# A routed feed-forward layer around attention: first layer's tiles grouped by batch, two batches' attention set between its last tiles

## The chip, the cores and the metric

One core of a Trainium2 chip. The metric is the time of one execution on the device in microseconds, median over several runs. Its engines are TensorE (PE in the profile, with its weight loads as PEld), VectorE (DVE), ScalarE (ACT), GpSimd (POOL) and the queue of SyncE (SP), which only issues transfers here.

## The reference

The input x is 4 batches of 256 tokens with 512 features, float32. Three steps are added to x in turn:

```python
x = x + 0.5 * ffn(layernorm(x), W_gate, b_gate, W_e, b_e)
x = x + attn(layernorm(x), Wqkv, bqkv, Wo, bo)
x = x + 0.5 * ffn(layernorm(x), W_gate, b_gate, W_e, b_e)

def ffn(x, W_gate, b_gate, W_e, b_e):        # 8 experts, 512 -> 512
    logits = x @ W_gate + b_gate
    _, top_idx = jax.lax.top_k(logits, 2)    # two experts for a token, equal weight
    y_all = relu(einsum('bsd,edh->bseh', x, W_e) + b_e)
    return take_along_axis(y_all, top_idx[..., None], axis=2).mean(axis=2)

def attn(x, Wqkv, bqkv, Wo, bo):             # one head of 128, within a batch
    q, k, v = split(x @ Wqkv + bqkv)
    return softmax(q @ k.T / sqrt(128)) @ v @ Wo + bo
```

Both feed-forward layers have the same weights. A token's attention needs the first layer's result for every token of its own batch, and for no other batch.

## The kernel before

The 1024 tokens are 8 row tiles of 128 (two for a batch); x stays in SBUF. Three phases follow one another.

**First layer.** For each batch, x is normalised, transposed, multiplied by the gate's weights (`gate`), and the two best experts of each token are found (`choose`). The 2048 pairs of token and expert are ranked within their expert by matmuls with a triangle of ones (`count`, `split_rank`). `tile_starts`, `slots` and `in_tiles` then put the pairs of one expert into tiles of 128 rows, expert after expert, over all batches together; `row_hots` and the matmuls of `token_list` turn this round into a list of tokens for each of NS = 23 tiles (16 would hold the pairs, 7 more allow for the partly filled last tile of each expert). `tokens` writes the list, and only then can the first gather start. `tile_experts` writes each tile's expert.

Each of the 23 tiles of `experts` is: a gather of 128 normalised rows from DRAM by POOL (`gather`), four transposes on PE, a split into a high and a low part (ACT's `hi_rows`, DVE's `lo_rows`), 12 matmuls of 128x512 (high by high, high by low, low by high), the bias on DVE (`bias`), ReLU on ACT (`relu`), and a scatter of the rows to `z_dram` (`scatter`). The expert weights (8 MB) stream in meanwhile; the last six half-loads wait until the first two gathers have landed (L401 to L404), and ACT and DVE split them in two parts (`split_hi`, `split_lo`). PE, ACT and DVE run tiles 8 to 19 in a loop.

**Attention.** All scatters of the first layer come first, since an expert's tiles hold tokens of all batches. Then DVE adds the two halves of z to x (`add_z`), takes the moments (`moments`), POOL raises the variance to the power -1/2 (`deviations`), DVE normalises, and PE, ACT and DVE pass through the four batches: transposes, `project_qk`, `project_v`, `scores`, maximum and exponential (`score_max`, `softmax`), `transpose_prob`, `mix_v`, `project_out`, `add_attention`. Every engine's order is written out by hand. Batch b's routing for the second layer (kind `g1`) stands between the steps of batches b+1 and b+2. The attention of one batch on PE is independent work for the waits of another. At the end of the phase an early list (`slots_early`, NA = 5 tiles filled from batches 0 to 2 alone) lets the second layer start before batch 3 is routed.

**Second layer.** As the first; batch 3's rows are transposed inside tile 0, gated after it, and its pairs listed by tile 3. Tiles from 5 on use the second list. At the end z is read back, added and stored.

PSUM has eight banks and all are used. `warm_up` issues matmuls whose results nobody reads. `WARM = [16, 10, 0]` stands behind the lists, `WARM_ATT = 14` ahead of the attention.

## Time and profile before

| | |
|---|---|
| time, median of 3 runs | 286.95 us (286.3 to 287.64) |
| time of the profiled execution | 283.61 us |
| its span, first to last instruction | 281.7 us |
| mean granted TensorE clock | 0.967 |
| PE busy | 240.1 us (85%) |
| DVE busy | 171.0 us (61%) |
| POOL busy | 120.4 us (43%) |
| ACT busy | 103.3 us (37%) |

The profiled execution took 1.9 us more than its span, which lie ahead of the first and behind the last instruction. All times below are microseconds from the start of the span. A busy PE here includes the unread matmuls of `warm_up`, so its share is not useful work alone; which engine sets the pace has to be read stage by stage.

### The profile page before, as it was taken

What the parts mean: (1) busy time and instruction counts of PE and PEld (TensorE: products, weight loads), DVE (VectorE), ACT (ScalarE), POOL (GpSimd) and SP (SyncE); (2) the same over time, 40 slices, a digit from 0 to 9 for tenths busy, and PEclk for the clock granted to TensorE, in tenths of its full rate; (3) what the DMA queues carried; (4) which work ended last, traced back from release to release, by engine and by line L of the source; (5) the groups of instructions that cost most, each with busy time, mean ns of one, the idle gap of its engine ahead of it and who ended that gap; (6) DMA issues with size and microseconds to landing.
All of it is one profiled execution on the core that took longest, in us unless ns stands there. A gap on an engine that the chain in (4) does not pass through costs nothing.

```text
span 281.7 us, 4837 instructions
## 1 busy us (share of the span) xinstructions
PE 240.1 (85%) x1302; PEld 178.2 (63%) x1303; DVE 171.0 (61%) x428; ACT 103.3 (37%) x184; POOL 120.4 (43%) x136
## 2 busy tenths in 40 slices
PE   6576788979999999989999968478969999999920
PEld 2342356758888888658786845246848888888710
DVE  3679947987344344775698785935843344443574
ACT  1888414554333333214244433013332433334200
POOL 4200373764656663324414400152076566664340
PEclk9999999999999999999999988689999999999995
DMA  7999249994444346353401011063056444454598
GB/s 241 387 391 411 79 131 353 416 381 129 147 151 137 132 150 198 108 154 100 149 3 74 20 58 74 1 176 124 0 168 203 134 134 147 152 147 152 213 370 315
DMA packets 22790, 49.38 MB, mean 175 GB/s; under 512 B 4333, under 2 KB 4973, under 8 KB 22513
## 3 DMA queue, kind: packets, MB, share of 16 engines
q1 hardware_dynamic: 13712, 26.55, 25.9%
q0 software_dynamic: 7360, 20.46, 22.8%
q10 hardware_dynamic: 1696, 2.11, 2.1%
q8 instruction: 11, 0.18, 0.3%
q14 instruction: 11, 0.08, 0.1%
HBM read 34.42 MB, written 18.35 MB: 187 GB/s over the span
## 4 chain that ended last, share of the span: by engine, by line
PE 58%; DMA 14%; DVE 12%; issue 5%; ACT 4%; SPq 2%; POOL 1%; DVEq 1%; POOLq 0%; ACTq 0%
PE qk_ps L845 17%; PE y_ps L845 17%; PE tp_ps L821 5%; PE qk_ps L916 5%; DMA xg<-xn_dram,tok 4%; DMA xg_late<-xn_dram,tok 4%; PE tp_ps L758 3%; DMA whi<-z_dram 3%; PE v_ps L925 3%; DMA raw<-in_L_ffn_W_e_dram 2%; DMA x<-in_L_attn_x_dram 2%; DVE row_hot L1144 2%; PE sp_ps L950 1%; DVE stats L1048 1%; PE rk_ps L745 1%
## 5 line engine op out<-in xcount | busy, mean ns | idle before, releaser
L514 POOL DMA_INDIRECT z_dram<-yrow,place x23 | 26.4, 1149 | 29.3 <-ACT yrow L637 26.7
L506 POOL DMA_INDIRECT xg<-xn_dram,tok x23 | 24.8, 1080 | 28.0 <-DVE tok L1193 20.8
L506 POOL DMA_INDIRECT xg_late<-xn_dram,tok x23 | 22.6, 981 | 33.0 <-DVE tok L1193 22.9
L1269 DVE TENSOR_TENSOR xt_lo_late<-tp_ps,xt_hi_late 128x512 fp32r<-128x512 f32 x23 | 15.9, 691 | 26.9 <-ACT xt_hi_late L627 26.9
L1269 DVE TENSOR_TENSOR xt_lo<-tp_ps,xt_hi 128x512 fp32r<-128x512 f32 x23 | 15.9, 691 | 24.2 <-ACT xt_hi L627 24.2
L637 ACT ACTIVATE yrow<-ypre 128x512 f32<-128x512 f32 x22 | 13.9, 632 | 43.4 <-DVE ypre L1277 43.4
L514 POOL DMA_INDIRECT z_dram<-xn,place x16 | 17.9, 1116 | 17.9 <-ACT xn L637 17.0
L499 POOL TENSOR_TENSOR rstd<-var_eps,neg_half 128x2 f32<-128x2 f32 x12 | 8.8, 737 | 32.4 <-DVE var_eps L1055 32.4
L358 DVE TENSOR_TENSOR wlo<-raw,whi 128x1024 fp32r<-128x1024 f32 x16 | 19.0, 1216 | 0.5 <-ACT whi L572 0.5
L637 ACT ACTIVATE xn<-ypre_late 128x512 f32<-128x512 f32 x14 | 8.8, 632 | 27.6 <-DVE ypre_late L1277 27.6
L1048 DVE BATCH_NORM_STATS2 stats<-x 128x6 f32<-128x512 f32 x24 | 15.7, 684 | 4.4 <-DMA x<-in_L_attn_x_dram 4.2
L627 ACT ACTIVATE xt_hi_late<-tp_ps 128x512 fp32r<-128x512 f32 x23 | 13.4, 583 | 11.3 <-PE tp_ps L821 11.3
L572 ACT ACTIVATE whi<-raw 128x1024 fp32r<-128x1024 f32 x16 | 16.3, 1048 | 1.6 <-DMA raw<-in_L_ffn_W_e_dram 1.6
L821 PE MATMUL tp_ps<-ident,xg_late 128*128 128x128 f32 x92 | 13.8, 274 | 3.2 <-DMA xg_late<-xn_dram,tok 3.2
L845 PE MATMUL y_ps<-whi,xt_hi 128*128 x48 | 14.5, 423 | 2.0 <-ACT xt_hi L627 1.1
L821 PE MATMUL tp_ps<-ident,xg 128*128 128x128 f32 x92 | 14.0, 275 | 2.1 <-DMA xg<-xn_dram,tok 2.1
L821 PEld LDWEIGHTS tp_ps<-ident,xg_late 128*128 128x128 f32 x92 | 11.0, 140 | 7.3 <-DMA xg_late<-xn_dram,tok 3.6
L627 ACT ACTIVATE xt_hi<-tp_ps 128x512 fp32r<-128x512 f32 x23 | 13.4, 581 | 6.2 <-PE tp_ps L821 6.2
L845 PE MATMUL y_ps<-whi,xt_hi_late 128*128 x48 | 14.4, 421 | 1.2 <-ACT xt_hi_late L627 1.2
L916 PE MATMUL qk_ps<-xt_att,wqkv 128*128 128x256 f32 x64 | 14.9, 386 | 0.4 <-ACT xt_att L611 0.4
L821 PEld LDWEIGHTS tp_ps<-ident,xg 128*128 128x128 f32 x92 | 11.0, 140 | 6.6 <-DMA xg<-xn_dram,tok 4.4
L745 PE MATMUL sp_ps<-ones 128*128 128x512 bf16 x50 | 14.2, 430 | 0.0
(177 smaller groups left out, 537.8 us busy)
## 6 DMA issues: line engine op xcount, KB each, us to landing
raw<-in_L_ffn_W_e_dram SPq DMA_DIRECT2D x16, 512.0 KB, 9.1
z_rows<-z_dram SPq DMA_DIRECT2D x6, 512.0 KB, 3.7
x<-in_L_attn_x_dram SPq DMA_DIRECT2D x8, 256.0 KB, 4.7
be_bc<-in_L_ffn_b_e_dram SPq DMA_DIRECT2D x2, 1024.0 KB, 12.0
xn_dram<-xn ACTq DMA_DIRECT2D x8, 256.0 KB, 2.1
whi<-z_dram SPq DMA_DIRECT2D x4, 512.0 KB, 5.4
wlo<-z_dram SPq DMA_DIRECT2D x4, 512.0 KB, 7.8
out_dram<-x SPq DMA_DIRECT2D x8, 256.0 KB, 3.3
```

Of the source, the lines that this page charges most:

```text
L358: eng.tensor_tensor(half(wlo, n), half(raw, n), half(whi, n).bitcast(F32), ALU.subtract).then_inc(done, 1)
L506: pool.indirect_dma_start(out=xg_at(f, t % XG), out_offset=None, in_=xn_dram[f][0:T - S if f and t < NA else T, :], in_offset=bass.Indirec ...
L514: pool.indirect_dma_start(out=z_dram[f][:, :], out_offset=bass.IndirectOffsetOnAxis(ap=place[:, t:t + 1], axis=0), in_=yrow_at(f, t % YB), ...
L572: act.activation(half(whi, n), half(raw, n), ACT.Copy).then_inc(hi_made, 1)
L627: act.activation(xt_hi_at(f, t % 2), tp_ps[(n0 + t) % 2][:], ACT.Copy).then_inc(tp_copied, 1)
L637: act.activation(yrow_at(f, t % YB), ypre_at(f, t % 2) if t < NY[f] else y_ps[t % 2][:], ACT.Relu, scale=HALF_MEAN).then_inc(yrow_made, 1)
L745: pe.matmul(bank[:], ones[:], ones[:].unsqueeze(1).broadcast_to([P, 4, P]), start=True, stop=True)
L821: last = pe.transpose(tp_ps[(n0 + t) % 2][:, c * P:(c + 1) * P], xg_at(f, t % XG)[:, c * P:(c + 1) * P], ident[:])
L845: last = pe.matmul(y_ps[t % 2][:], rows[:, c * P:(c + 1) * P], w[:, bass.ds(e * WE + c * H, H)], start=(n == 0), stop=(rows is lo and c == ...
L916: last = pe.matmul(qk_ps[:, j * S:(j + 1) * S], wqkv[:, c, j * D:(j + 1) * D], xt_att[:, c, :], start=(c == 0), stop=(c == NC - 1))
L1048: read.append(step(dve.bn_stats(stats[:, s + i, :], x[:, TB * b + i, :])))
L1269: dve.tensor_tensor(xt_lo_at(f, t % 2), tp_ps[(n0 + t) % 2][:], xt_hi_at(f, t % 2).bitcast(F32), ALU.subtract).then_inc(xt_made, 1)
```

## The change

- The first layer's pairs go into tiles by groups: first the tiles that batch 0 opens, expert after expert, then those that batch 1 opens beyond them (a pair fills up the expert's open tile first), then batch 2, then batch 3. `group_slots(0, 3)` computes this for three batches ahead of the last batch's `choose`, and `group_slots(3, 4)` for the last behind it. They replace `tile_starts(0)` and `slots(0)`. `tile_experts(0)` compares with the ends of 32 groups instead of 8.
- The rows of z for a batch are read as soon as the scatters of its groups have landed; SP waits on counts in `sent_rows`. They are read by 256 KB into two row slots of `xn`, one after the other.
- The attention of batch 0 starts in tile 16 of the first layer and that of batch 1 in tile 20, in pieces on PE, ACT and DVE inside and behind tiles. Its buffers lie in `xt_gate` and in the last batch's part of x, which SP loads again from the input afterwards.
- The first layer is written out in full on PE, ACT and DVE, with no loop.
- After the first layer come batch 2's attention, the second layer's routing of batches 0, 1 and 2, and batch 3's projections; the early list stands ahead of batch 3's softmax, so its gathers go out beside the rest of batch 3's attention. `project_out(3)` is then the last step before the second layer's first tile.
- The unread matmuls go: 14 + 2 ahead of the attention, 10 behind the early list.

The core of the diff:

```diff
+    EARLY = 2
+    START = (16, 20)
...
-        WARM = [16, 10, 0]
-        WARM_ATT = 14
+        WARM = [16, 0, 0]
...
-        HEADS, STEP = (E, NA), 6
+        HEADS, STEP = (NS, NA), 6
...
+                def attention_inside(t):
+                    for b in range(EARLY):
+                        if t == START[b]:
+                            transpose_xn("att", b)
+                        if t == START[b] + 1:
+                            project_v(b)
+                            scores(b)
+                        if t == START[b] + 2:
+                            transpose_prob(b)
+                        if t == START[b] + 3:
+                            project_out(b)
+
+                def attention_behind(t):
+                    for b in range(EARLY):
+                        if t == START[b]:
+                            project_qk(b)
+                        if t == START[b] + 2:
+                            mix_v(b)
...
             experts(0)
+            transpose_xn("att", 2)
+            project_out(1)
+            project_qk(2)
+            project_v(2)
+            scores(2)
+            transpose_xn("g1", 0)
+            transpose_prob(2)
+            mix_v(2)
+            project_out(2)
+            gate(1, 0)
+            transpose_xn("g1", 1)
+            transpose_logits(1, 0)
+            gate(1, 1)
+            count(1, 0)
+            transpose_logits(1, 1)
+            transpose_xn("g1", 2)
+            transpose_xn("att", 3)
+            count(1, 1)
+            gate(1, 2)
+            project_qk(3, 0, 1)
+            transpose_logits(1, 2)
+            project_qk(3, 1, 2)
+            project_v(3)
+            count(1, 2)
+            scores(3)
             token_list(1)
+            transpose_prob(3)
+            mix_v(3)
+            project_out(3)
             experts(1)
...
+            def group_slots(first, end):
+
+
+                n = end - first
+                cols = slice(JB * first, JB * end)
+                pairs = JB * n
+                counts = group_at[:, first + 1:end + 1, 1, :]
+                dve.tensor_tensor(above[:, 0:n], upto[:, first:end, :].unsqueeze(3).broadcast_to([P, n, E, NT]),
+                                  thresh[:].unsqueeze(1).broadcast_to([P, n, E, NT]), ALU.is_gt
+                                  ).then_inc(rank_read, n)
+                dve.wait_ge(rank_read, B + end if end == B else B - 1 + n)
+                link(dve.tensor_reduce(counts, above[:, 0:n], AX_X, ALU.add))
+                link(dve.tensor_tensor(group_new[:, first:end, :], counts, group_at[:, first:end, 1, :], ALU.subtract))
+                link(dve.tensor_tensor_scan(ends[:, 0:end, :].rearrange("p b e -> p (b e)"),
+                                            group_new[:, 0:end, :].rearrange("p b e -> p (b e)"),
+                                            zeros(end * E), 0.0, ALU.add, ALU.add))
...
+                link(dve.tensor_tensor(
+                    hot, onehot[:, TB * first:TB * end].rearrange("p t k e -> p (t k) e").unsqueeze(2)
+                    .broadcast_to([P, pairs, 2 * end, E]),
+                    group_at[:, 1:end + 1].rearrange("p b c e -> p (b c) e").unsqueeze(1)
+                    .broadcast_to([P, pairs, 2 * end, E]), ALU.mult))
+                link(dve.tensor_reduce(of_pair, hot, AX_X, ALU.add))
...
+            split_rank(0, 2)
+            group_slots(0, B - 1)
             choose(0, 3)
-            split_rank(0, 2)
             row_hots(0, 2)
-            tile_starts(0)
-            slots(0)
+            split_rank(0, 3)
+            group_slots(B - 1, B)
+            in_tiles(0, slot_t[:])
+            row_hots(0, 3)
             tokens(0)
             tile_experts(0)
...
             experts(0)
+            normalise("att", 2)
+            dve.wait_ge(x_att, TB)
+            moments("g1", 0)
+            add_attention(1)
+            normalise("g1", 0)
+            dve.wait_ge(x_att, TB * 2)
+            moments("g1", 1)
+            add_bv(2)
+            normalise("g1", 1)
+            score_max(2)
+            add_z(6)
+            add_z(7)
+            moments("att", 3)
+            invert_sums(2)
+            add_attention(2)
+            dve.wait_ge(x_att, TB * 3)
+            moments("g1", 2)
+            normalise("att", 3)
+            choose(1, 0)
+            normalise("g1", 2)
+            split_rank(1, 0)
+            row_hots(1, 0)
+            choose(1, 1)
+            split_rank(1, 1)
+            row_hots(1, 1)
+            choose(1, 2)
+            add_bv(3)
             slots_early()
+            row_hots(1, 2)
+            score_max(3)
             tokens(1)
+            tile_experts(1)
+            invert_sums(3)
+            add_attention(3)
             dve.wait_ge(x_att, TB * B)
+            moments("g1", 3)
+            normalise("g1", 3)
             leave_early()
             experts(1)
```

## Rows read from the trace of the kernel before

**Rows 1.** The page, granted clock in 40 slices of the span.

```profile
PEclk9999999999999999999999988689999999999995
```

**Rows 2.** Windows: length, busy of each engine, granted clock, DMA share, GB/s.

```profile
118.14:129.40 11.26, 10.00 (x59) 7.23 (x57) 7.85 (x19) 2.52 (x5) 3.06 (x5) 1.00 0.60 188
129.40:162.60 33.20, 32.73 (x194) 26.34 (x193) 25.53 (x65) 14.10 (x35) 12.80 (x12) 1.00 0.16 58
162.60:190.79 28.19, 19.45 (x118) 11.97 (x117) 18.69 (x77) 6.17 (x14) 5.48 (x6) 0.82 0.25 77
190.79:210.70 19.91, 16.38 (x106) 11.91 (x104) 13.30 (x48) 7.03 (x13) 7.41 (x8) 1.00 0.28 89
```

**Rows 3.** Windows around the clock's fall (columns as in rows 2).

```profile
165.10:167.83 2.73, 0.28 (x4) 0.04 (x2) 2.55 (x9) 1.02 (x4) 0.70 (x1) 0.96 0.00 0
167.83:171.10 3.27, 3.27 (x14) 3.18 (x15) 1.29 (x13) 1.55 (x3) 0.00 (x0) 0.51 0.32 122
```

**Rows 4.** Timeline of DVE and POOL, first list: start, length, instruction, idle before.

```profile
22.30 0.22 DVE L1082 TENSOR_REDUCE logit<-g_ps 128x16 f32<-128x64 f32 x1
...
23.61 0.18 DVE L1111 TENSOR_TENSOR picked<-onehot,rk_ps 128x32 f32<-128x32 bf16 x1
...
25.07 0.22 DVE L1082 TENSOR_REDUCE logit<-g_ps 128x16 f32<-128x64 f32 x1
...
32.40 0.33 DVE L1152 TENSOR_TENSOR passed<-iota_t,incl 1x184 f32<-1x184 f32 x1
...
32.79 1.18 POOL L506 DMA_INDIRECT xg<-xn_dram,tok  x1 [20.78 <-DVE tok L1193]
...
33.22 3.47 DVE L358 TENSOR_TENSOR wlo<-raw,whi 128x1024 fp32r<-128x1024 f32 x3
...
34.27 3.25 POOL L506 DMA_INDIRECT xg<-xn_dram,tok  x1 [0.31 <-issue]
```

**Rows 5.** Timeline of DVE and ACT: operations by size, and the steps of a softmax.

```profile
142.16 0.69 DVE L1384 TENSOR_REDUCE smax<-sp_ps 128x2 f32<-128x512 f32 x1 [0.53 <-PE sp_ps L934]
...
143.09 0.47 ACT L685 ACTIVATE prob<-sp_ps,nmax 128x256 f32<-128x256 f32 x1 [1.09 <-DVE nmax L1385]
...
146.54 0.60 ACT L727 ACTIVATE pt<-sp_ps 128x512 f32<-128x512 f32 x1
...
177.44 0.36 DVE L1218 TENSOR_TENSOR picked_a<-onehot,bounds 128x192 f32<-128x192 bf16 x1
```

**Rows 6.** The chain that ended last: start, length, engine and line.

```profile
39.95 5.31 DMA raw<-in_L_ffn_W_e_dram
...
111.75 2.78 PE qk_ps L845 x12
...
140.38 0.87 PE tp_ps L758 x8
...
142.12 3.65 PE qk_ps L916 x16
145.78 0.44 PE sp_ps L942 x4
146.21 1.79 PE v_ps L925 x16
...
149.74 0.86 PE y_ps L962 x2
```

**Rows 7.** Timeline of DVE and POOL ahead of the second layer.

```profile
176.28 0.18 DVE L1111 TENSOR_TENSOR picked<-onehot,rk_ps 128x32 f32<-128x32 bf16 x1
...
179.22 0.68 DVE L1144 TENSOR_TENSOR row_hot<-iota_r,slot_r 128x512 bf16<-128x512 bf16 x1
...
180.95 1.28 DVE L1048 BATCH_NORM_STATS2 stats<-x 128x6 f32<-128x512 f32 x2
...
184.17 0.74 POOL L499 TENSOR_TENSOR rstd<-var_eps,neg_half 128x2 f32<-128x2 f32 x1
...
185.04 1.00 DVE L1075 TENSOR_SCALAR xn<-x,mv,rstd 128x512 f32<-128x512 f32 x2 [1.77 <-POOL rstd L499]
```

More of the change, by code:

```diff
@@ L315, in xn_slot @@
         def xn_slot(n):
-            return n if n < NT else n % XN
+            if n < NT:
+                return n
+            return n % TB if n < NT + EARLY * TB else (n + TB) % XN
         def xn_at(n):
@@ L1150, in tile_experts @@
                 first, tiles, _, _ = LISTS[n]
-                ends = bounds[0:1, 1, :] if n == 1 else incl[0:1, :]
-                link(dve.tensor_tensor(passed[:, 0:tiles], iota_t[0:1, 0:tiles].unsqueeze(2).broadcast_to([1, tiles, E]),
-                                       ends.unsqueeze(1).broadcast_to([1, tiles, E]), ALU.is_ge))
-                link(dve.tensor_reduce(eid_f[:, first:first + tiles], passed[:, 0:tiles], AX_X, ALU.add))
-                dve.tensor_scalar(eid[:, first:first + tiles], eid_f[:, first:first + tiles], float(E - 1), None,
-                                  ALU.min).then_inc(eid_made, 1)
+                part = slice(first, first + tiles)
@@ new lines, in tile_experts @@
+                if n == 0:
+                    hot = row_hot[0:1].rearrange("p j r -> p (j r)").bitcast(F32)[:, 0:NS * B * E].rearrange(
+                        "p (t e) -> p t e", t=NS)
+                    passing = ends[0:1].rearrange("p b e -> p (b e)")
+                else:
+                    hot = passed[:, 0:tiles]
+                    passing = bounds[0:1, 1, :] if n == 1 else incl[0:1, :]
+                of_all = hot.shape[2]
+                link(dve.tensor_tensor(hot, iota_t[0:1, 0:tiles].unsqueeze(2).broadcast_to([1, tiles, of_all]),
+                                       passing.unsqueeze(1).broadcast_to([1, tiles, of_all]), ALU.is_ge))
@@ L1274, in bias, with attention @@
                     dve.wait_ge(exp_done, done)
-                    if used is not None:
+                    if f == 0:
+                        if t >= YB:
+                            dve.wait_ge(scattered[t % YB], 16 * (t // YB))
+                    else:
                         dve.wait_ge(yrow_made, used)
-                    dve.tensor_tensor(ypre_at(f, t % 2), y_ps[t % 2][:],
+                    dve.tensor_tensor(ypre_at(f, t), y_ps[t % 2][:],
                                       be_bc[:, bass.ds(e * H, H)], ALU.add).then_inc(ypre_made, 1)
                 halves = list(range(LO_AHEAD, 2 * E)) if f == 0 else []
+                def attention(t):
+                    if t == START[0] - 4:
+                        add_z(0)
+                    if t == START[0] - 3:
+                        add_z(1)
+                    if t == START[0] - 2:
+                        moments("att", 0)
+                    if t == START[0] - 1:
+                        normalise("att", 0)
+                        add_bo(0)
+                    if t == START[0]:
+                        add_z(2)
+                        score_max(0)
+                    if t == START[0] + 1:
+                        add_bv(0)
+                        add_z(3)
+                    if t == START[0] + 2:
+                        invert_sums(0)
+                        moments("att", 1)
+                    if t == START[1] - 1:
+                        normalise("att", 1)
+                        add_attention(0)
+                    if t == START[1]:
+                        add_z(4)
+                        score_max(1)
+                    if t == START[1] + 1:
+                        add_bv(1)
+                        add_bo(1)
+                        add_z(5)
+                    if t == START[1] + 2:
+                        moments("att", 2)
+                        invert_sums(1)
                 def tile(t):
@@ new lines, in add_z @@
+                for m in range(TOP_K * i, TOP_K * (i + 1)):
+                    last = m - TOP_K * (NT - TB)
+                    if last < 0:
+                        dve.wait_ge(z_in[m % 2], 16 * (m // 2 + 1))
+                    else:
+                        dve.wait_ge(z_last[last], 16)
+                    if m % TOP_K:
+                        dve.wait_ge(z_added, m)
+                    dve.tensor_tensor(x[:, i, :], x[:, i, :], z_row(m), ALU.add).then_inc(z_added, 1)
+            bo_steps = {}
@@ new lines, in invert_sums, with add_attention @@
+            def invert_sums(b):
+                dve.wait_ge(prob_made, TB * (b + 1))
+                link(dve.reciprocal(pinv[:], psumrow[:]))
+            def add_attention(b, first=0, end=TB):
+                for q in range(first, end):
+                    i = TB * b + q
+                    if b < EARLY:
+                        dve.wait_ge(dve_step, bo_steps[i])
+                    else:
+                        dve.wait_ge(bo_added, i - TB * EARLY + 1)
+                    dve.wait_ge(wo_done, i + 1)
+                    dve.scalar_tensor_tensor(out=x[:, i, :], in0=wo_bank(b, q)[:], scalar=pinv[:, q:q + 1],
+                                             in1=x[:, i, :], op0=ALU.mult, op1=ALU.add).then_inc(x_att, 1)
```

612 lines of the change are left out of this document (312 added, 300 removed).

## The prediction

> **What bounds the kernel now.** I read the page's clock row first, then a table of windows, the chain that ended last, and the timelines of the stretches that the change touches. In the clock row [rows 1] the reader is to see one valley in the middle of the span. The windows [rows 2] place it. From 129.40 to 162.60 PE is busy 32.73 of 33.20 us: three batches' attention, each filling the other's waits, at full clock. Ahead of it, from 118.14 (the first layer's last matmul) to 129.40, its 10.00 busy us contain 16 unread warm-up matmuls. Behind it, from 162.60 to 190.79 (the end of the second layer's tile 0), PE is busy 19.45 of 28.19 us at a mean clock of 0.82, ten warm-ups included; the work there is half of one batch's attention, the early list and one tile. So some 20 us of the 72.65 us from 118.14 to 190.79 are latency. The first layer's later tiles are bound by PE: 2.78 us for 12 matmuls [rows 6], with 0.44 us of transposes between, and nothing else on the chain. The first list is bound by DVE: until 32.79, when the first gather goes out, one DVE operation follows the other [rows 4].
>
> **The sum's base** is the profiled execution, 283.61 us. The median of the runs is 286.95, 3.3 us above it; the difference found below is added to the median. A difference of 0.5% is 1.4 us, about what a measurement can tell here.
>
> **The first list grows.** All of it stands on DVE's chain to the first gather. An operation on 192 elements takes 0.36 us, one on 512 takes 0.69 [rows 5]; on that line 576 elements cost 0.76, 256 cost 0.43, 64 cost 0.23, and the smallest ones 0.18 [rows 4]. Each has some 0.03 us to the next.
> - `group_slots(0, 3)`: 192 elements compared and summed (2 x 0.39), a product of 12 pairs by 6 groups by 8 experts = 576 elements and its sum (2 x 0.79), seven small ones with a scan (7 x 0.20): 3.8 us.
> - `group_slots(3, 4)`: 64 elements twice (0.5), 256 elements twice (0.9), seven small ones (1.4): 2.8 us.
> - Out go `tile_starts(0)` and `slots(0)`, whose own part is 1.1 us (an estimate: two operations on 128 elements and four small ones).
>
> Net 5.5 us. `choose` (22.30 to 23.61, 1.3 us) and rank with row marks (23.61 to 25.07, 1.5 us) [rows 4] change places and keep their costs. `tile_experts(0)` also grows, from 184 to 736 elements, twice, about 1.4 us, but behind the gather's issue. Is the delay hidden later? The last six half-loads of weights wait for the first two gathers, and the chain has one of them at 39.95 for 5.31 us [rows 6]; they move with the list. So the whole first layer moves: +5.5. Bounds: +3.5 if the second gather slips ahead of DVE's weight splits and the loads go out earlier; +6.8 if the splits' own delay of 1.4 is added.
>
> The second of these bounds is visible in one pair of rows: the gather issued at 34.27 took 3.25 us, the one before it 1.18, and DVE split weights for 3.47 us from 33.22 [rows 4]. The Trainium skill, page "SBUF — State Buffer", the section "SBUF: two separate sides", has GpSimd write its descriptors through a port pair that VectorE holds for a whole instruction in its fast modes; that agrees with the 3.25 us. By that rule the second gather ends only with the later splits, and the sum would be 1.4 us higher; by the row alone it may pass as the first one did.
>
> **Attention between the tiles.** One batch on PE is, by the chain [rows 6]: transposes 0.87, query and key 3.65, value 1.79, scores 0.87, probabilities transposed 0.44, mix 0.87, projection 2 x 0.86: 10.2 us. Batch 0 brings all, batch 1 all but the mix and projection (2.6) by the end of tile 22: 17.8 us. Following DVE's order through tiles 15 to 20 I find two stalls. In tile 16 the second transpose waits for `lo_rows(17)`, which stands behind `bias(15)`, `normalise` (1.00, [rows 7]) and `add_bo` (two of 0.65): 1.1 us. In tile 20 it waits likewise behind `normalise` and `add_attention`: 1.2 us. Everything else is covered: maximum 0.69 and two exponentials of 0.47 [rows 5] lie beside 3.2 us of matmuls. Are z's rows there? I counted the reference's routing on its inputs: the tiles opened end at 8, 12, 16 and 19, so batch 2 is complete with tile 15 and its rows are first added in tile 20. Tile 22 ends 20.2 us later than without the pieces (17.8 + 2.3, and 0.1 of small waits).
>
> **From tile 22 to the second layer's tile 0.** PE's work there, piece by piece in the order of the diff with the prices above (gates 0.57 and lists 0.6 as estimates): 33.6 us. I followed the five engines' orders step by step; PE waits
> - 2.7 ahead of batch 2's transposes: `moments` (1.28 and some small ones) starts on DVE only after `add_bv`, `add_bo` and `add_z(5)` of tile 21, then POOL's 0.74 and the normalisation follow [rows 7];
> - 1.9 for batch 2's probabilities, since `score_max(2)` stands behind `add_bv(2)` and `normalise("g1", 1)`; 1.2 in its two copies by ACT (0.60 and about 0.4, [rows 5]);
> - 2.9 for `choose(1, 0)` and `choose(1, 1)`, behind four `add_z`, two `moments`, and `add_attention`;
> - 3.1 for the early list: `slots_early` takes 2.94 (176.28 to 179.22, [rows 7]) and starts only when batch 3's value is projected and `add_bv(3)` done;
> - 1.6 and 1.2 for batch 3's probabilities and copies, with the softmax now behind the list;
> - 1.9 around tile 0, where batch 3's moments and normalisation, begun after `project_out(3)`, are no longer early.
>
> These make 16.5, and 1.2 us of small waits: 51.3 us where before 72.65 passed. DVE is busy 39 of the 51: it is the engine that sets this stage. The first gather of the second layer is covered, as meant. Saved: 21.3.
>
> **Clock.** Before, PE was nearly idle for 2.73 us (165.10 to 167.83), and the next 3.27 us of work ran at 0.51 of full clock [rows 3], half of them lost: 1.6 us. The new order has two such gaps, 2.7 and 3.1 us, and no unread matmuls to bridge them, each followed by work on the path: 2 x 1.6 = +3.3 (bounds: 0, and 7 if the clock stays down through the sparse part).
>
> **Sum:** +5.5 + 20.2 - 21.3 + 3.3 = +7.6 us. The second layer's tiles 1 to 4 keep their chain of waits, 16.38 busy of 19.91 us [rows 2]. 283.61 becomes 291.2, and the median 286.95 becomes 294.5. Own range of this case: 289 to 300.
>
> **Rivals.**
> - *The new order hides its own waits.* For it: the dense stretch, where hand-ordered pieces left 0.5 us idle in 33.2 [rows 2]. Against it: DVE had 7.7 us to spare there, and here has 39 busy us in 51. If half of the 20 us (16.5 waits and 3.3 clock) goes, the time is 284.5; if all, 275. It decides, as faster than before by 1.4, once 9 of these 20 are gone.
> - *The clock holds* across both gaps: 291.2.
> - *The clock stays down* from the gate of batch 0 to `project_out(3)`: some 15 us of PE work, spread over 25, at half clock; half of the extra 15 falls into waits, so +7 instead of +3.3 and the later tiles start cold: 300 to 302. For it: one gap was enough before. Against it: work came back to 1.00 after each. The Trainium skill, "TensorE: Matmul & The Clock Gate", Part 1, says that the gate follows how busy the engine was lately; the fall after 2.73 idle us agrees, and it would make a stage as sparse as this the wrong place to drop warm-ups.
> - *The growth of the list is swallowed*, because the weights set the pace of tiles 2 to 6: 289. Against it: their loads are released by the gathers.
> - *The interleaving does not work*: rows of z land late, each `add_z` stalls DVE and then PE. With two row slots and a read back issued only after the addition before last, four late reads of 3 us make 305. The counts speak against it.
>
> **Chances.** Forecast 0.45, order hides its waits 0.20, clock holds 0.13, clock stays down 0.10, growth swallowed 0.08, interleaving fails 0.04. Faster: the second case and an edge of the mild ones, 0.22. Within 0.5%: 0.08. Slower: 0.70. The range takes half of the faster case and the cold one: 282 to 302.
>
> **What would show it.** The first gather at 38.2 and not 32.8; tile 22 ending near 144; pieces of attention inside tiles 16 to 22 with PE busy over 95%; gaps of 2 to 3 us ahead of batch 2's transposes and of the early list's matmuls, with granted clock 0.5 behind them; tile 0 of the second layer ending near 198. I am wrong if the gather leaves before 36, or if DVE idles long after tile 22 while PE is dense, or if tile 0 ends before 190.

## The result, and the profile after

The changed kernel takes 304.18 us (median of 4 runs, 303.28 to 306.0), the kernel before 286.72 us beside it. The ratio is 1.070, with a 95% interval of 1.063 to 1.077; the two medians alone give 1.061, the two profiled executions 1.070. Which of the two is nearer isn't settled, but both are far beyond the spread of the runs. Below, ratios leave out executions in a slower state that any kernel here sometimes falls into, while medians are of all runs. The prediction had 294.5 us and a range up to 302: the direction is right, the size is not. The profiled execution took 303.42 us; its span of 301.3 us is 19.6 longer than before, where the forecast had 7.6.

The page's clock row of the changed kernel, in the place of [rows 1]:

```profile
PEclk9998699999999979999979686959999999999995
```

One valley became many: the first list (slices 4 and 5), tile 16 (slice 15), and four stretches after tile 22 (slices 21, 23, 24 with 25, and 27). The windows, in the place of [rows 2]: first tile 12's first matmul to the end of tile 22, then to the end of the second layer's tile 0, then its next tiles.

```profile
89.21:147.74 58.53, 55.25 (x278) 44.94 (x277) 32.55 (x60) 19.40 (x40) 21.66 (x21) 0.97 0.35 109
147.74:210.96 63.22, 45.56 (x236) 31.59 (x236) 39.29 (x135) 15.98 (x35) 14.56 (x15) 0.81 0.21 68
210.96:230.30 19.34, 15.76 (x103) 11.59 (x102) 13.30 (x48) 6.43 (x12) 6.91 (x7) 1.00 0.33 107
```

In the middle row PE is busy for 45.56 of 63.22 us at a clock of 0.81; DVE's 39.29 us are what the prediction had (39). The cold stretches by themselves, each with the granted clock in the third column from the right:

```profile
106.60:110.00 3.40, 2.98 (x9) 2.56 (x10) 0.32 (x2) 0.60 (x1) 1.55 (x2) 0.53 0.44 149
151.10:154.30 3.20, 3.18 (x10) 2.40 (x11) 2.00 (x6) 1.19 (x2) 1.26 (x2) 0.52 0.20 53
164.90:171.30 6.40, 5.24 (x11) 2.91 (x12) 3.20 (x9) 2.07 (x4) 0.70 (x1) 0.50 0.22 82
178.80:185.00 6.20, 5.67 (x33) 4.22 (x34) 4.81 (x25) 2.78 (x5) 0.00 (x0) 0.50 0.23 87
195.80:202.20 6.40, 4.50 (x10) 2.69 (x11) 0.69 (x5) 1.67 (x6) 2.00 (x2) 0.50 0.29 82
```

That is 25.6 us at the lower of the clock's two levels, with 21.6 us of PE work in them, where before one such stretch held 3.27 us of work [rows 3], and one more the ten unread matmuls behind the early list. What PE waited for from tile 22 to tile 0 (total, times, longest):

```profile
PE tp_ps L841 <- DVE xn L1193: 4.5, 3, 2.5
PE sp_ps L1060 <- ACT prob L769: 3.9, 2, 2.3
PE v_ps L895 <- ACT mark_a L683: 2.4, 1, 2.4
PE g_ps L856 <- DVE logit L1200: 2.0, 1, 2.0
PE sp_ps L1068 <- ACT pt L777: 1.4, 2, 0.7
```

These are the waits of the forecast, in its places: ahead of batch 2's transposes (2.5, forecast 2.7), for the probabilities of batches 2 and 3 (2.3 and 1.6; forecast 1.9 and 1.6), for the early list (2.4; forecast 3.1), for `choose` (2.0 and 0.5 us; forecast 2.9 together). In all PE is idle for 17.7 us of this stretch, in sum the forecast's 17.7; what the forecast lacked is mostly the speed of the work between the waits.

Where the 19.6 us of the span are, by the same landmarks in both traces:

| | before | after | difference | forecast |
|---|---|---|---|---|
| start to tile 12's first matmul | 82.6 | 89.2 | +6.6 | +5.5 |
| tile 12 to the end of tile 22 | 35.6 | 58.5 | +23.0 | +20.2 |
| end of tile 22 to the end of tile 0, second layer | 72.65 | 63.22 | -9.4 | -18.0 (-21.3 + 3.3) |
| the rest | 90.9 | 90.3 | -0.6 | 0 |

The stretch behind tile 0 is the same work in all variants of the changed kernel, and its length lay between 90.3 and 92.5 us in their traces. Differences of a microsecond or two between single traces are therefore not read where nothing was changed.

The second row's surplus begins in tile 16. DVE's timeline of the changed kernel there, then PE's:

```profile
98.01 1.49 DVE L1539 TENSOR_TENSOR x<-x,xn 128x512 f32<-128x512 f32 x2 [1.73 <-DMA xn<-z_dram]
...
104.07 1.00 DVE L1193 TENSOR_SCALAR xn<-x,mv,rstd 128x512 f32<-128x512 f32 x2 [0.41 <-POOL rstd L564]
104.99 1.29 DVE L1545 TENSOR_TENSOR x<-x,bo_bc 128x512 f32<-128x512 f32 x2
106.19 0.68 DVE L1437 TENSOR_TENSOR xt_lo<-tp_ps,xt_hi 128x512 fp32r<-128x512 f32 x1
```

```profile
104.67 0.66 PE L841 MATMUL tp_ps<-ident,xn 128*128 128x128 f32 x4 [0.50 <-DVE xn L1193]
107.02 1.08 PE L841 MATMUL tp_ps<-ident,xn 128*128 128x128 f32 x4 [1.69 <-DVE xt_lo L1437]
107.76 2.05 PE L933 MATMUL y_ps<-whi,xt_lo 128*128 x4
```

The chain is read backwards: four matmuls took 2.05 us and not some 1.1 because the clock had fallen; the transposes ahead of them waited 1.69 us for `lo_rows(17)`; that stood behind the normalisation and `add_bo`, as forecast, but all of it was late, since DVE had waited 1.73 us for rows of z. Their read went out at 93.69, only when the addition before had freed the one buffer it needs.

### The profile page after: what moved, and what is told of

It reads as the page before. It is cut to its first block, busy times and chain, and to the rows that moved or that the text cites. A ratio compares the mean times of both kernels' runs of the same rounds, so it can differ in the third digit from the quotient of the medians.

```text
span 301.3 us, 4702 instructions
## 1 busy us (share of the span) xinstructions
PE 245.4 (81%) x1276; PEld 181.1 (60%) x1277; DVE 180.0 (60%) x454; ACT 104.1 (35%) x184; POOL 116.1 (39%) x133
## 4 chain that ended last, share of the span: by engine, by line
PE 48%; DVE 19%; DMA 15%; issue 6%; ACT 5%; POOL 2%; SPq 2%; DVEq 1%; POOLq 0%; ACTq 0%
PE qk_ps L933 14%; PE y_ps L933 12%; DMA be_bc<-in_L_ffn_b_e_dram 5%; PE tp_ps L907 4%; PE tp_ps L841 3%; DMA wlo<-z_dram 3%; PE qk_ps L1031 2%; PE g_ps L1031 2%; PE v_ps L1043 2%; DMA xg<-xn_dram,tok 2%; DVE xn L1193 2%; PE sp_ps L1068 2%; DVE stats L1166 1%; DMA xn<-z_dram 1%; DMA x<-in_L_attn_x_dram 1%
## 5 line engine op out<-in xcount | busy, mean ns | idle before, releaser
L571 POOL DMA_INDIRECT xg<-xn_dram,tok x23 | 26.8, 1166 | 34.2 <-DVE tok L1328 26.3
L703 ACT ACTIVATE yrow<-yrow 128x512 f32<-128x512 f32 x22 | 13.9, 632 | 41.6 <-DVE yrow L1448 41.6
L579 POOL DMA_INDIRECT z_dram<-xn,place x16 | 16.5, 1030 | 18.2 <-ACT xn L703 17.2
L841 PE MATMUL tp_ps<-ident,xn 128*128 128x128 f32 x80 | 14.6, 330 | 9.8 <-DVE xn L1193 5.0
L564 POOL TENSOR_TENSOR rstd<-var_eps,neg_half 128x2 f32<-128x2 f32 x12 | 8.8, 735 | 33.6 <-DVE var_eps L1173 33.6
L841 PEld LDWEIGHTS tp_ps<-ident,xn 128*128 128x128 f32 x80 | 11.0, 168 | 14.4 <-DVE xn L1193 6.5
L907 PE MATMUL tp_ps<-ident,xg_late 128*128 128x128 f32 x92 | 13.7, 273 | 2.8 <-DMA xg_late<-xn_dram,tok 2.8
```

What stands on the lines that cost most here:

```text
L571: pool.indirect_dma_start(out=xg_at(f, t % XG), out_offset=None, in_=xn_dram[f][0:T - S if f and t < NA else T, :], in_offset=bass.Indirec ...
L579: pool.indirect_dma_start(out=z_dram[f][:, :], out_offset=bass.IndirectOffsetOnAxis(ap=place[:, t:t + 1], axis=0), in_=yrow_at(f, t % YB), ...
L703: act.activation(yrow_at(f, t % YB), ypre_at(f, t) if t < NY[f] else y_ps[t % 2][:], ACT.Relu, scale=HALF_MEAN).then_inc(yrow_made, 1)
L841: last = pe.transpose(tp_ps[n % 2][:, c * P:(c + 1) * P], xn_at(m)[:, c * P:(c + 1) * P], ident[:])
L907: last = pe.transpose(tp_ps[use_no[(f"exp{f}", t)] % 2][:, c * P:(c + 1) * P], xg_at(f, t % XG)[:, c * P:(c + 1) * P], ident[:])
```

## The experiments

The kernel before was run beside each group of four; its runs there lie between 281.69 and 288.19 us, so times of different groups are compared through their ratio to it. Unless a sentence below says so, nothing of the computation is left out.

**1. The kernel before with a longer first list.** Operations of the sizes of `group_slots` are added to DVE's chain (192, 192, 576, 576 elements and small ones ahead of `choose(0, 3)`, 256, 256 and small ones behind it), results unread.

```diff
+            pad([192, 192, 8, 24, 8, 576, 576, 24, 24, 12, 12])
             choose(0, 3)
...
+            pad([32, 8, 256, 256, 12, 12])
             slots(0)
             tokens(0)
```

> The kernel before with 17 unused VectorE operations of the sizes of the groups' arithmetic set ahead of the first list (11 before the last batch's choice, 6 ahead of the slots), about 5.5 us of VectorE. If the first layer moves with its list, +5.5 us (291.3 to 292.5). If the weight loads set the pace of the first tiles and swallow the delay, under +2 us.

The first gather moved by 4.96 us (32.79 to 37.75), the end of tile 22 by 4.9 (118.14 to 123.04), the span from 281.7 to 286.7. Time 290.9 us, ratio 1.019 (1.008 to 1.030). In this trace every microsecond ahead of the first gather is one in the end: nothing swallows it. Its clock row dips to 7 in slice 5, where the row of before has 9, so the changed kernel's dip in the first list comes with the longer list.

**2. The same, with `tile_experts` longer by two operations of 552 elements.**

```diff
+            for n in (552, 552):
+                link(dve.tensor_tensor(scratch[:, 0:n], ...))
             tile_experts(0)
```

> As the run with the longer list, and two operations of 552 elements on one partition, 1.4 us, between the list and the tiles' experts. If the weight splits behind them hold up the second gather, and with it the last weight loads, this adds another 1.0 to 1.4 us (+6.6 in all, what the first layer of the changed kernel shows). If what stands behind the first gather's issue is covered, it adds under 0.3 us.

Tile 22 ended at 124.96, 6.8 us later than before and 1.9 later than in experiment 1; the ratio, 1.016 (1.006 to 1.026), doesn't separate the two. The way was not the expected one. POOL's gathers in this kernel:

```profile
38.20 1.37 POOL L506 DMA_INDIRECT xg<-xn_dram,tok  x1 [26.38 <-DVE tok L1193]
39.88 0.95 POOL L506 DMA_INDIRECT xg<-xn_dram,tok  x1 [0.31 <-issue]
41.13 3.31 POOL L506 DMA_INDIRECT xg<-xn_dram,tok  x1 [0.30 <-issue]
```

DVE's three splits ran from 40.14 to 43.6, so the second gather passed in 0.95 us and the third took 3.31. In the changed kernel the splits began at 39.82 and the second gather, at 39.91, took the blow:

```profile
39.91 4.22 POOL L571 DMA_INDIRECT xg<-xn_dram,tok  x1 [0.31 <-issue]
```

A gather that is issued beside the splits is held over all three of them: in both kernels, and in the kernel before (34.27, 3.25 us), it ends 0.8 us behind the last split. The Trainium skill, "SBUF — State Buffer", section "SBUF: two separate sides", has a VectorE operation with two inputs in SBUF hold a shared port pair for the whole instruction against a GpSimd operation that reads SBUF. These splits have two such inputs, and the traces agree, with 3.31 and 4.22 us beside 0.95, if a gather counts as such an operation; that no run here separates.

The layer was late by about as much in both kernels, but not for the same reason. In the changed kernel tile 1's transposes waited 0.97 us for the second gather's rows. Here the second gather passed and released the last weight loads at 43.46, ahead of the third gather, and tile 2's transposes waited for that one:

```profile
49.22 0.66 PE L821 MATMUL tp_ps<-ident,xg 128*128 128x128 f32 x4 [2.27 <-DMA xg<-xn_dram,tok]
```

(Experiment 7 shows this second way again.) So experiment 2 doesn't reproduce the changed kernel's delay. It does show that the prediction's lower bound of +3.5, where the second gather slips ahead of the splits and the loads go out earlier, isn't a gain. The changed kernel's own delay behind the first gather is read by comparing traces: from its first gather to tile 12's first matmul it takes 51.2 us, and 50.6 to 52.5 in experiments 4 to 6 and 9 to 11, against 49.3 to 49.8 in the kernel before and experiments 1, 3 and 12.

**3. The kernel before without its unread matmuls** between the layers: the 14 + 2 ahead of the attention and the 10 behind the early list, the same that the change drops.

```diff
-        WARM = [16, 10, 0]
+        WARM = [16, 0, 0]
...
-            warm_up(WARM_ATT)
...
-            warm_up(2)
```

> The kernel before without the 16 unread matmuls ahead of its attention and the 10 behind the early list. If the clock was a part of the price of the change, +2 to +5 us, with stretches at half clock behind 122 and 185. If the engine's waits alone set the pace there, within 1 us.

Time 289.71 us beside 287.07, ratio 1.015 (1.004 to 1.026); the span grew from 281.7 to 285.6. In the clock row the stretch of the first list is untouched and two places are new or deeper, at the start of the attention and ahead of the second layer:

```profile
PEclk9999999999999999959999998659999999999995
```

Without any of the rest of the change, this one edit costs 2.6 us by the medians and 3.9 by the spans. From the end of tile 22 to the end of tile 0 it is 78.2 us and not 72.65; the first layer and the rest came out 1.6 us shorter with nothing changed in them.

**4. The changed kernel with unread matmuls in every gap in which the clock fell.** 7 in tile 16 and as many in tile 20, 10 ahead of batch 2's transposes, 13 around its probabilities, 13 around `gate(1, 1)`, 20 from the early list to the mix of batch 3.

```diff
             experts(0)
+            pe.wait_ge(x_att, TB)
+            warm_up(10, rk_ps)
             transpose_xn("att", 2)
...
+            warm_up(9, rk_ps)
             transpose_prob(2)
+            warm_up(2, rk_ps)
             mix_v(2)
...
+            warm_up(8, qk_ps)
             gate(1, 1)
...
             scores(3)
+            warm_up(10, qk_ps)
             token_list(1)
+            warm_up(6, qk_ps)
             transpose_prob(3)
```

> The changed kernel with 5 to 10 unread matmuls in each of the gaps that its trace shows ahead of a fall of the clock (in tiles 16 and 20, ahead of batch 2's transposes, of its probabilities, of the second gate, of the third transposes, of the early list and of batch 3's probabilities). Theory of the clock: five cold stretches cost 10 us between them, and 6 to 10 us come back (294 to 298). Rival: VectorE's chain sets the pace and the half clock lies beside it; under 3 us come back (over 301).

Time 296.41 us, ratio 1.037 (1.025 to 1.049): 7.8 of the 17.5 us came back, or 3.3 of the 7.0 per cent, though the order of the real work is the same on every engine. The stage between the layers, as the middle row of the windows above:

```profile
147.36:202.38 55.02, 48.82 (x293) 31.22 (x292) 39.31 (x135) 15.64 (x35) 14.53 (x15) 1.00 0.25 78
```

55.0 us instead of 63.2, DVE's busy time unchanged, the clock at 1.00. The cost of the clock in this stage is therefore 8.2 us; the forecast had 3.3.

**5. Rows of z a tile sooner.**

```diff
-                    if t == START[0] - 4:
+                    if t == START[0] - 5:
                         add_z(0)
```

> The changed kernel with batch 0's rows of z added one tile sooner (in tile 11 and not in tile 12), so that their row slot is free and the next read goes out some 2.8 us earlier; all else as in the changed kernel, nothing left out. Theory: in tile 16 PE waited 1.7 us more than I had worked out and then ran 3.4 us at half clock because DVE had waited 1.73 us for the second pair of z rows. Then add_z(1) waits for nothing, the transposes of batch 0 wait about 1 us in tile 16, the clock keeps 1.0 there, tile 22 ends at 144.5 to 146 and not 147.7, and the time is 1.5 to 3 us under the changed kernel's: 301 to 302.7. Rival: the wait of tile 16 comes from lo_rows(17) standing behind the normalisation and add_bo, whenever the rows land: then tile 22 still ends at 147 or later, and the time falls by less than 1 us. Second rival: batch 0's own rows are not there a tile sooner, and the stall only moves: no gain or a loss up to 1 us.

301.39 us, ratio 1.056 (1.049 to 1.063). This interval only touches that of the changed kernel, and by the medians alone (301.39 over 284.7, 1.059 beside 1.061) next to nothing was gained, so the traces have to tell. From tile 12 to the end of tile 22 it is 55.8 us and not 58.5; in tile 16 PE waited once, for 1.22 us (forecast 1.1), and the clock stayed up:

```profile
104.08 0.60 PE L841 MATMUL tp_ps<-ident,xn 128*128 128x128 f32 x4
105.89 0.63 PE L841 MATMUL tp_ps<-ident,xn 128*128 128x128 f32 x4 [1.22 <-DVE xt_lo L1437]
106.28 1.17 PE L933 MATMUL y_ps<-whi,xt_lo 128*128 x4
```

So the late rows were the cause of the surplus of tile 16, and the rival falls. What is left, 20.3 us over before, is the forecast's 20.2, and in its parts: PE is busy 18.0 us longer than before (forecast 17.8) and waits 2.3 us in two places (forecast 2.3).

**6. Batch 3's softmax ahead of the early list**, on DVE, ACT and PE (ACT's line isn't shown).

```diff
             add_bv(3)
+            score_max(3)
             slots_early()
             row_hots(1, 2)
-            score_max(3)
...
             scores(3)
+            transpose_prob(3)
             token_list(1)
-            transpose_prob(3)
             mix_v(3)
```

> The changed kernel with batch 3's maximum and exponentials ahead of the early list on DVE and ACT, and its transposed probabilities ahead of token_list on PE; nothing left out. It undoes the order that lets the first gather of the second layer go out beside the rest of the attention. Theory: the list alone is 3 us of DVE work and PE has nothing meanwhile, so whichever goes first, the other waits; the two cold stretches behind 178.8 and 195.8 come from these two gaps. With the softmax first, PE has the mix and projection while DVE makes the list, one of the gaps closes, and tile 0's first product starts 1 to 3 us earlier unless its gather, which goes out later by about 1.2 us, sets its start: the time is 301 to 304 (0 to 3 us less). Rival: the early gather is what matters, its landing sets the start of tile 0; then the time rises by 1 to 3 us, to 305 to 307.

301.93 us, ratio 1.062 (1.053 to 1.071), against 1.070 (1.063 to 1.077): an overlap, so the times alone leave it open. In the trace tile 0 of the second layer starts its last product 59.7 us after the end of tile 22, and 62.0 us in the changed kernel (that product then ran at half clock here, so the ends are only 61.7 and 63.2). PE waited there for the list for 1.05 us and not 2.44. The gather that the change lets go early is not what tile 0 waits for here:

```profile
200.20 0.60 PE L907 MATMUL tp_ps<-ident,xg_late 128*128 128x128 f32 x4
201.63 1.19 PE L933 MATMUL y_ps<-whi,xt_hi_late 128*128 x4 [0.83 <-ACT xt_hi_late L693]
```

The transposes of its rows follow `project_out(3)` with no wait, as in the changed kernel. The order that the change chose for the list buys nothing and costs 1.5 to 2.3 us in this trace, with the clock as low as it is here; experiment 10 tries it with the clock held.

**7. The last six loads released by the first gather.**

```diff
-            for s in range(2):
-                sp.wait_ge(gathered[s], 16)
+            sp.wait_ge(gathered[0], 16)
```

> The changed kernel, but the last six half-loads of expert weights wait for the first gather alone and not for the first two; nothing left out. Theory: the first layer's delay is 6.6 us and not 5.5 because the second gather, blocked for 4.2 us while DVE splits weights, releases those loads at 46.55 and not at 45.5; released by the first gather they go out near 40 to 41, tile 4 to 6 are no longer late, and tile 12's first product starts 2 to 4 us earlier (85 to 87 and not 89.2), the time 2 to 4 us less. Rival: what holds tiles 2 to 6 is their gathers behind the splits and the broadcast of the tiles' experts and biases, not the loads; then tile 12 starts within 1 us of 89.2 and the time stays within 1 us; the gathers beside the loads may even take longer, with a loss up to 2 us.

305.48 us, ratio 1.072 (1.064 to 1.080). The loads went out at 42.85 instead of 46.55, and tile 16's first transposes came at 107.89 instead of 104.67 (0.9 of it because this run's first gather was at 38.96). The theory falls. The rival's last clause had the cause, that the gathers take longer beside the loads, though not its size:

```profile
45.33 1.07 PE L932 MATMUL y_ps<-wlo,xt_hi 128*128 x4
50.83 1.12 PE L906 MATMUL tp_ps<-ident,xg 128*128 128x128 f32 x4 [4.43 <-DMA xg<-xn_dram,tok]
51.60 2.06 PE L932 MATMUL y_ps<-whi,xt_lo 128*128 x4
```

The loads went out ahead of the second gather's rows; PE waited 4.43 us for these, and then ran at half clock. That gather left POOL at 45.06 and could be used at 50.8; in the changed kernel it left at 44.13 and was there at 46.5. With 3 MB of weights sent out ahead of it a gather of 256 KB takes 5.7 us and not 2.4. The wait for two gathers keeps the loads behind these rows.

**8. All four edits**, 4 to 7, together.

> The changed kernel with all four edits: z rows a tile sooner, batch 3's softmax ahead of the early list, the loads released by the first gather, and unread matmuls in every gap in which the clock fell. Nothing of the computation is left out. Sum of the theories: 296.4 with the unread matmuls alone, less 1.0 for z (its cold stretch is already counted), less 1 to 2 for the order, less 2 to 4 for the loads: 290 to 293, still 3 to 6 us above the kernel before. Rival, that the edits all take the same waits away: 294 to 297. If it lands under 286 the changed order would have been worth making, and my reading that DVE's work sets the stage is wrong.

295.83 us, ratio 1.038 (1.031 to 1.045): no better than experiment 4 alone. Tile 22 ended at 148.10 (147.36 in experiment 4) though z came sooner: the loads took away what that gave.

**9. Experiments 4 and 5 together.**

> The changed kernel with the two repairs together: unread matmuls in every gap in which the clock fell, and z rows a tile sooner; nothing of the computation is left out. Theory: these two are the whole of what my prediction missed. Unread matmuls alone brought the time from 304.2 to 296.4, z rows alone to 301.4 (1.056 of the kernel before against 1.070); the first cold stretch is in both, so together 293.5 to 295.5, ratio 1.024 to 1.034, which is the 294.5 of the prediction. Rival: something else is left, or they take away the same wait: over 296. Second rival: under 292, then the latencies that I had summed are partly covered.

294.22 us, ratio 1.039 (1.031 to 1.046). The median lies in the expected range, the ratio does not: the runs of the kernel before that it counts have a mean of 283.3 us in this group. That the median is close to the prediction's 294.5 is luck. The prediction has 3.3 us for the clock in it, and here the clock is held; the span of 293.0 is 11.3 us above before, where the forecast without its clock term says 4.3. To tile 12 it is +7.0, from tile 12 to 22 +20.7 (with z's rows in time the unread matmuls have no gap to bridge there), and from tile 22 to the end of tile 0

```profile
145.80:200.83 55.03, 48.82 (x292) 31.23 (x292) 39.33 (x135) 15.65 (x35) 14.54 (x15) 1.00 0.25 78
```

or -17.6 for a forecast of -21.3; the rest +1.3. Of the 48.82 busy us, 13.7 are unread matmuls (the rows of `ones` in its groups by line, 33 for 8.1 us and 23 for 5.6), so 35.1 are work, for 33.6 forecast; 19.9 are waits, covered or not, for 17.7. This also checks the price of the clock: in the changed kernel PE was busy 45.56 us with the same work, 10.5 more than 35.1, and idle 2.2 less than 19.9, which leaves 8.2.

**10. The same, with the softmax order of 6.**

```diff
             scores(3)
-            warm_up(10, qk_ps)
+            warm_up(7, qk_ps)
+            transpose_prob(3)
+            warm_up(6, qk_ps)
             token_list(1)
-            warm_up(6, qk_ps)
-            transpose_prob(3)
-            warm_up(2, qk_ps)
             mix_v(3)
```

> As after_warmed_z, with batch 3's maximum and exponentials ahead of the early list as well, and the six loads again released by both of the first gathers; nothing left out. Theory: all_and_warmed came out at 1.038, not better than unread matmuls alone, because its loads went out beside the second gather, which landed 4.4 us late; without that edit the order of the softmax is worth 1 to 2.7 us (it was 2.7 us in the stage without the unread matmuls): 291.5 to 294. Rival: with the clock held, the gather of tile 0 sets its start, and the softmax's place is worth nothing or costs 1 us: 294 to 296. Either way I expect it to stay above the kernel before by 2% or more.

294.06 us, ratio 1.037 (1.029 to 1.045): no difference from experiment 9 that these runs can tell. The stage is 54.55 us for 55.03, at a clock of 0.97 for 1.00. In this order tile 0 does wait for its gather, which leaves later, and the clock falls behind it:

```profile
193.81 0.66 PE L911 MATMUL tp_ps<-ident,xg_late 128*128 128x128 f32 x4 [1.36 <-DMA xg_late<-xn_dram,tok]
195.30 1.73 PE L937 MATMUL y_ps<-whi,xt_hi_late 128*128 x4 [0.83 <-ACT xt_hi_late L693]
```

So this is the expectation's rival. The reason that the change gave for its order, the early gather, holds once the clock is held, and takes back most of what the other order gives: half a microsecond is left, in one pair of traces.

**11. Experiment 9 with POOL's `add_bo(3)` on 8 of 512 columns**; the other 504 columns of that addition are left out.

```diff
-                    pool.tensor_tensor(x[:, i, :], x[:, i, :], bo_bc[:], ALU.add).then_inc(bo_added, 1)
+                    n = H if b != 3 else 8
+                    pool.tensor_tensor(x[:, i, 0:n], x[:, i, 0:n], bo_bc[:, 0:n], ALU.add).then_inc(bo_added, 1)
```

> As after_warmed_z, but POOL's add_bo(3) adds the output bias to 8 columns of batch 3's rows instead of 512: the other 504 columns of that part of the computation are left out. Theory: DVE sets the stage between the layers, and the two small operations of choose(1, 0) that run beside POOL's 2.52 us take 1.9 us where they take 0.4 elsewhere; with POOL's work gone they take 0.4 again, and tile 0 of the second layer starts 1.0 to 1.5 us earlier. Rival: that part of DVE's chain has slack (the unread matmuls cover it), and the start of tile 0 moves by less than 0.4 us, though the operations get short. Third: they stay long, then POOL is not their cause.

292.96 us, ratio 1.034 (1.027 to 1.042), with 1.039 for experiment 9: not told apart by the times. From the end of tile 22 to the last product of tile 0, 52.9 us and not 53.9. The two operations in the changed kernel's trace, beside POOL's, and then in this one's:

```profile
176.74 0.62 DVE L1208 TENSOR_TENSOR onehot<-iota_e,topi 128x32 bf16<-128x32 f32 x1
177.28 1.30 DVE L1214 TENSOR_TENSOR place_at<-topi 128x2 f32<-128x2 uint32 x2
```

```profile
176.04 2.52 POOL L611 TENSOR_TENSOR x<-x,bo_bc 128x512 f32<-128x512 f32 x2
```

```profile
169.53 0.19 DVE L1225 TENSOR_TENSOR onehot<-iota_e,topi 128x32 bf16<-128x32 f32 x1
169.65 0.23 DVE L1231 TENSOR_TENSOR place_at<-topi 128x2 f32<-128x2 uint32 x2
```

1.92 us became 0.42, and 1.0 of these 1.5 us reached the start of tile 0. Both parts of the theory stand: POOL's addition slows DVE's small operations, and DVE's chain sets most of the time at this place.

**12. The kernel before with 10 unread matmuls in its one long gap.**

```diff
             transpose_logits(1, b - 2)
+            pe.wait_ge(x_att, TB * b)
+            warm_up(10, qk_ps)
             transpose_prob(b)
```

> The kernel before with 10 unread matmuls in its one long gap, ahead of transpose_prob(3), where PE was idle for 2.5 us and then ran 3.3 us at 0.51 of full clock; nothing left out. Theory: the fall of the clock costs 1.6 us there, and this gives it back, less what the unread matmuls reach past the end of the gap: 1.0 to 1.8 us less than before, ratio 0.994 to 0.997. Rival: DVE sets the work behind this gap (choose and the lists), so that PE's slow stretch was covered: within 0.5 us of the kernel before.

Ratio 1.004 (0.996 to 1.012), medians 285.21 and 285.87 us: no difference. The reason is neither of the two. The edit did what it was meant to: batch 3's transposed probabilities found a full clock (0.66 us instead of 1.11), and `token_list(1)` came 1.4 us sooner, counted from tile 22. But then:

```profile
177.54 0.76 PE L809 MATMUL v_ps<-mark_a,row_hot 128*128 128x10 bf16 x12 [3.73 <-ACT mark_a L617]
178.15 4.43 PE L745 MATMUL sp_ps<-ones 128*128 128x512 bf16 x10
183.28 1.11 PE L821 MATMUL tp_ps<-ident,xg_late 128*128 128x128 f32 x4 [0.70 <-DMA xg_late<-xn_dram,tok]
185.22 2.07 PE L845 MATMUL y_ps<-whi,xt_hi_late 128*128 x4 [0.83 <-ACT xt_hi_late L627]
187.09 1.91 PE L845 MATMUL y_ps<-wlo,xt_hi_late 128*128 x4
```

In both kernels the ten unread matmuls behind the list run cold (4.43 us), after the wait of 3.7. Before, the clock was up again when tile 0 began at 185.40; here tile 0 began 1.6 us earlier, counted from tile 22, and ran at half clock, so that it ended 1.4 us later. What one gap gave back, the next one took. Why the clock came back later here than there isn't shown.

## Why the prediction was wrong

- *What bounds the kernel, and DVE as the engine that sets the stage*: right as far as it was tried. DVE's 39.3 busy us were forecast as 39, and at the one place that experiment 11 tried, 1.0 of 1.5 us of DVE's chain is one of the stage. The rival "the new order hides its own waits" falls: PE was idle 17.7 us, as forecast.
- *The first list, +5.5*: the first gather was at 38.04 for a forecast of 38.2; the term is right up to there. The layer came 6.6 us late: behind the first gather another 1.4 us are lost, which stood in the prediction as a bound and was the better value (51.2 us to tile 12, where 49.3 to 49.8 passed without the longer `tile_experts`). The splits began 1.35 us later after the first gather than before, and the second gather was held for 4.22 us, from its start. Experiment 1 confirms that the growth ahead of the gather isn't hidden. The rival of a swallowed growth falls. The rule that the prediction took from the page of the skill is the one for VectorE's fast modes; that the splits ran in one is shown by no row. The sum doesn't rest on it, and the hold of the gather is measured either way.
- *Attention between the tiles, +20.2*: 17.8 for the pieces and 2.3 for the stalls are right once the rows of z are in time (+20.3 in experiment 5). The step that failed is "Are z's rows there?": I counted when the rows were complete, not when the buffer that they are read into was free, though the prediction's last rival names exactly this serial read. One such wait of 1.73 us on DVE cost 2.7 us, a part of it through the clock.
- *Tile 22 to tile 0, -21.3*: -17.6 with the clock held. 1.5 us are PE work priced too low, 1.5 us lie beside POOL's `add_bo(3)`, which I had costed at DVE's undisturbed durations; of which 1.0 reached tile 0 in experiment 11 (batch 1's normalisation for its second routing, 1.73 us for two operations where [rows 7] have 1.00, lies beside `add_bo(2)` in the same way, with no experiment on it); the rest isn't resolved.
- *Clock, +3.3*: this is the term that failed most. It is 8.2 us in this stage by experiment 4 (63.2 against 55.0). I had counted the two gaps near 3 us, each followed by as much cold work as before [rows 3]. There were four cold stretches in this stage and one in tile 16. Waits of 2.3 us, and of 2.0 us among sparse small matmuls, had one behind them as well, and in tile 16 one of 1.7; and in three of the five the cold stretch was over 6 us long, twice that of before. Why these were longer isn't shown. In two of them (from 164.9 and 195.8) the slow work is itself broken by waits of 0.5 to 0.7 us, but the third, from 178.8, is nearly dense (5.67 busy of 6.20 us). The prediction's case "the clock stays down", +7 at a chance of 0.10, is nearest to what happened, if not in one piece: the clock came back between, but never for long. Its rule from the Trainium skill ("TensorE: Matmul & The Clock Gate", Part 1: the gate follows how busy the engine was lately) had pointed there, and the traces of experiments 3 and 4 agree with it (the clock fell where unread matmuls were taken out and kept 1.00 where they were put in).

The sum in spans: 1.1 (list), 2.8 (rows of z), 3.7 (stage at full clock), 4.9 (its clock), -0.6 (the rest) are the 12 us by which 19.6 is more than 7.6. The medians differ by less, 9.7, since the profiled execution of before lay 3.3 us under its median and that of the changed kernel 0.8.

As for the change: its grouping of tiles works as described, and even repaired it stays 3 to 4% above the kernel before. No run showed a version faster than that one. Some 18 us of PE work went ahead of tile 22 and about as much came away behind it; what was left to gain were the waits between the layers, and the one batch's work that remains beside DVE's 39 us is too little for PE to fill them. That last sentence is a reading of the windows, not an experiment: a variant with more of the attention inside the first layer wasn't tried.

## What to carry to other kernels

When work is moved out of a stage, count what the rest leaves PE to do there. Here the waits of 2 us and more between the layers were paid twice, once as waits and once in the slow work behind them. Price the clock by how much work stands in the sparse stretch, not by the number of its gaps: PE was busy for 18.6 us at half speed between the layers, which cost 8.2 us. Before dropping unread matmuls make that removal by itself (experiment 3: 2.6 us by the medians). And when asking whether data is there, follow the buffer it lands in and the read's issue, not only the moment at which it is complete.

## What the runs showed of the hardware beyond that

- Small operations of DVE took 0.62 and 1.30 us (the latter two of them) beside POOL's 2.52 us of additions, and 0.19 and 0.23 without these.
- A gather of 256 KB behind six weight loads took 5.7 us from its issue's end to its use (experiment 7) and 4.8 us (experiment 2), 2.4 without them ahead.
- A gather issued beside three splits of 128x1024 on DVE took 3.25 to 4.22 us and ended 0.8 us behind the last of them, 0.95 us without. One issued 0.26 us ahead of the first split passed in 0.95.
- Bridging one gap can leave the following, unchanged work colder than it was (experiment 12: tile 0's first four matmuls 2.07 us, 1.18 before).
